# Two layers of cross attention and expert mixtures on one core: routing products in another PSUM bank and place, gathers behind clearing, expert weights split earlier

## The chip, the cores and the metric

The kernel runs on one core of a Trainium2 chip. The metric is the device time of one execution in microseconds. The engines of the core work side by side and wait for each other by semaphores: TensorE (PE in the rows, its weight loads are PEld), VectorE (DVE), ScalarE (ACT), GpSimd (POOL), and SyncE (SP), which only issues transfers.

## The reference

16 batches of 512 tokens with 256 channels go through two layers. Each layer adds a cross attention over 64 context rows and then a mixture of eight experts:

```
x = x + L0_xattn(layernorm(x), ctx, ctx)             # 16 heads of 16
x = x + L0_ffn(layernorm(x))     # router: top 1024 tokens per expert, silu(x Wu) Wd, scatter-add
x = x + L1_xattn(layernorm(x), ctx, ctx, masks)      # the same with two masks
x = x + L1_ffn(layernorm(x))     # every token through all 8 experts, silu(gate) * up, weighted sum
```

In the first mixture a softmax over eight router logits gives each token a gate per expert; each expert takes the 1024 tokens that want it most, so 8 experts times two halves of 512 tokens make 16 groups. Experts of a pair share the up projection (256 to 682), each has its own down projection (682 to 256).

## The kernel before, in words

Nearly every product runs in float32 as three passes: each operand is split into a rounded high part (ACT or DVE) and the remainder (DVE), and PE adds high×high, high×low and low×high (`three_passes`, L143 to L145). There is no scheduler. Each engine has its own program, written out by hand, and the order in that program is the order of execution; `wait_ge(sem, n)` stops everything behind it on that engine.

**Attention** (function `attention`, run once per layer, here 0 and 1). It is pipelined over batches. In the body of batch b, PE does the scores of b (`scores`, L570 to L589, two halves c), the transposes of the input of b+1 (`turn_input`, L530), the output projection of b-1 (`outputs`, L619), the queries of b+1, then four tiles t of weighted values (`weighted_values`, L604) with the maxima products of b+1 between them (`maxima`, L559), the transposes of the new normalised rows of b-1 (`turn_new`, L676), the router logits of b-1 (`route`, L638, eight products), the transposes of the attention result of b (`turn_attention`, L616), and the transposes of the maxima of b+1 (`turn_maxima`, L566). DVE divides each weighted-value tile by its sum (`normalise`, L856 and L858, which signals `av_taken`), reduces the maxima (`maxima`, L844, `s_taken`), copies the turned maxima out (`maxima_copy`, L849, `max_ready`), copies the router logits (`router_copy`, L863, `lg_out`) and takes the remainder of the attention result (`attention_lo`, L868, `a_lo`). ACT takes the exponentials (L736) and high parts (L724 input, L762 attention result). `scores` of the next batch waits for `max_ready`; `turn_attention` waits for the last `av_taken`; `turn_maxima` waits for the last `s_taken`. PSUM has eight banks: weighted values alternate between 6 and 7, outputs use 6 for tiles 0 and 1 and 7 for tiles 2 and 3, the router logits use 6.

**First mixture** (`expert_choice_mixture`). The loop `iterations` runs over q = 0 to 3, one up projection and two experts each; the first three passes share one loop body and the last is written apart. Each q has four groups j of 512 tokens. PE does up(j) (36 products of 512 columns in six chunks f) and, behind it, down(j-1) (72 products of 256 columns); inside up(j), ahead of chunk 2, it turns the rows of group j+1 (`turn`, L1370). POOL gathers the rows by indirect DMA (`gather`, L1316 index copy, L1323) and adds the results back (`add`, L1337), all from one in-order queue. ACT does `hidden`: a Silu per chunk (L1436) and the high parts (L1442 to L1445). DVE takes the remainders (L1493 to L1499), the input's high and low parts (`rows_lo`, L1468 to L1472) after the first remainder of the group before, and the scaled outputs (L1506). There is one raw buffer for a down matrix (`wd`) and two slots for its split form; SP loads the next matrix once `wd_ready` says that DVE has finished the last split (L1296). ACT makes the high part (`down_weights`, L1429), DVE the remainder (L1483). Slot 0 of the next q is split at the end of a q, slot 1 just behind group 0 of its own q.

## Time and profile before

| | us |
|---|---|
| median of 3 runs | 2418.28 (2417.42 to 2419.39) |
| profiled execution, its own time | 2419.39 |
| its span in the profile | 2417.3 |
| PE busy | 2208.7 (91%) |
| DVE busy | 1457.4 (60%) |
| ACT busy | 862.7 (36%) |
| POOL busy | 367.9 (15%) |

The span runs in stages: attention of layer 0 until about 437 us, expert choice to 553 us, the first mixture to 864 us, attention of layer 1 until 1321 us, and the second mixture to the end. Matmuls are pipelined, so a busy PE is not PE at its peak; the starts of the weight loads (PEld) show best when PE goes on to the next piece of work. A bracket at the end of a row tells how long the engine stood idle before it and what released it.

### The profile page before, as it was taken

What the parts mean: (1) busy time and instruction counts of PE and PEld (TensorE: products, weight loads), DVE (VectorE), ACT (ScalarE), POOL (GpSimd) and SP (SyncE); (2) the same over time, 40 slices, a digit from 0 to 9 for tenths busy, and PEclk for the clock granted to TensorE, in tenths of its full rate; (3) what the DMA queues carried; (4) which work ended last, traced back from release to release, by engine and by line L of the source; (5) the groups of instructions that cost most, each with busy time, mean ns of one, the idle gap of its engine ahead of it and who ended that gap; (6) DMA issues with size and microseconds to landing.
All of it is one profiled execution on the core that took longest, in us unless ns stands there. A gap on an engine that the chain in (4) does not pass through costs nothing. (4 is left out here: it accounts for less than half of the span.)

```text
span 2417.3 us, 40461 instructions
## 1 busy us (share of the span) xinstructions
PE 2208.7 (91%) x15335; PEld 1919.7 (79%) x15335; DVE 1457.4 (60%) x3137; ACT 862.7 (36%) x1210; POOL 367.9 (15%) x352
## 2 busy tenths in 40 slices
PE   7999999546999949999996899999999999999998
PEld 4888888325889837788875788888888888888887
DVE  6787876685544447777774774455445554554454
ACT  2455554124544414454442522222222222222222
POOL 3111110105666421111110400000000000000000
PEclk9999999768999969999998999999999999999999
DMA  2121211204444321111112300000000000000000
GB/s 75 53 69 61 78 61 45 65 0 120 100 82 81 44 50 45 61 62 63 57 53 70 114 27 27 27 27 27 1 26 27 27 27 27 27 27 27 27 10 9
DMA packets 110137, 115.05 MB, mean 48 GB/s; under 512 B 16080, under 2 KB 98768, under 8 KB 110032
## 3 DMA queue, kind: packets, MB, share of 16 engines
q1 hardware_dynamic: 97744, 96.49, 12.6%
q0 software_dynamic: 12288, 17.05, 4.2%
q8 instruction: 80, 1.31, 0.2%
q14 instruction: 25, 0.20, 0.0%
HBM read 62.92 MB, written 50.59 MB: 47 GB/s over the span
## 5 line engine op out<-in xcount | busy, mean ns | idle before, releaser
L1882 DVE TENSOR_TENSOR zmix_hid<-zmix_act_gate,psum 128x1024 f32<-128x1024 f32 x128 | 156.4, 1222 | 372.2 <-issue 346.7
L143 PE MATMUL psum<-zmix_wd_hi,zmix_hid_hi 128*128 128x256 f32 x1024 | 289.5, 283 | 2.3 <-DVE zmix_acc L1873 2.3
L145 PE MATMUL psum<-zmix_wd_hi,zmix_hid_lo 128*128 128x256 f32 x1024 | 289.8, 283 | 0.0
L144 PE MATMUL psum<-zmix_wd_lo,zmix_hid_hi 128*128 128x256 f32 x1024 | 289.7, 283 | 0.0
L1833 ACT ACTIVATE zmix_hid_hi<-zmix_hid 128x1024 fp32r<-128x1024 f32 x128 | 135.5, 1058 | 393.3 <-PE psum L145 285.5
L1825 ACT ACTIVATE zmix_act_gate<-psum 128x1024 f32<-128x1024 f32 x128 | 131.6, 1028 | 379.1 <-PE psum L145 379.1
L604 PE MATMUL psum<-att_v_cur,att_probs 128*128 128x96 f32 x2048 | 250.0, 277 | 3.1 <-ACT att_probs L736 3.1
L604 PEld LDWEIGHTS psum<-att_v_cur,att_probs 128*128 128x128 f32 x2048 | 239.1, 192 | 12.0 <-ACT att_probs L736 4.0
L1887 DVE TENSOR_TENSOR zmix_hid_lo<-zmix_hid,zmix_hid_hi 128x1024 fp32r<-128x1024 f32 x128 | 157.8, 1233 | 135.2 <-ACT zmix_hid_hi L1833 134.2
L1873 DVE SCALAR_TENSOR_TENSOR zmix_acc<-psum,zmix_weight,zmix_acc 128x256 f32<-128x256 f32 x512 | 211.7, 476 | 1.6 <-PE psum L145 1.6
L143 PE MATMUL psum<-zmix_xT_hi,zmix_wg_hi 128*128 128x512 f32 x512 | 201.9, 394 | 10.9 <-DVE zmix_xT_lo L1862 10.9
L143 PE MATMUL psum<-zmix_xT_hi,zmix_wu_hi 128*128 128x512 f32 x512 | 200.3, 391 | 4.9 <-DVE zmix_hid L1882 4.7
L143 PEld LDWEIGHTS psum<-zmix_wd_hi,zmix_hid_hi 128*128 128x128 f32 x1024 | 196.0, 191 | 8.7 <-issue 2.0
L144 PE MATMUL psum<-zmix_xT_lo,zmix_wg_hi 128*128 128x512 f32 x512 | 201.6, 394 | 0.0
L145 PE MATMUL psum<-zmix_xT_hi,zmix_wg_lo 128*128 128x512 f32 x512 | 199.9, 390 | 0.0
L144 PEld LDWEIGHTS psum<-zmix_wd_lo,zmix_hid_hi 128*128 128x128 f32 x1024 | 196.0, 191 | 4.8
L144 PE MATMUL psum<-zmix_xT_lo,zmix_wu_hi 128*128 128x512 f32 x512 | 199.8, 390 | 0.0
L145 PE MATMUL psum<-zmix_xT_hi,zmix_wu_lo 128*128 128x512 f32 x512 | 199.7, 390 | 0.0
L145 PEld LDWEIGHTS psum<-zmix_wd_hi,zmix_hid_lo 128*128 128x128 f32 x1024 | 196.0, 191 | 0.0
L736 ACT ACTIVATE att_probs<-psum 128x512 f32<-128x512 f32 x256 | 132.3, 603 | 151.8 <-PE psum L589 79.5
L844 DVE TENSOR_REDUCE att_s_max<-psum 128x8 f32<-128x512 f32 x256 | 163.7, 682 | 30.8 <-PE psum L559 29.5
L143 PEld LDWEIGHTS psum<-zmix_xT_hi,zmix_wg_hi 128*128 128x128 f32 x512 | 97.2, 190 | 28.0 <-DVE zmix_xT_lo L1862 11.1
(295 smaller groups left out, 4502.2 us busy)
## 6 DMA issues: line engine op xcount, KB each, us to landing
x<-att_x_new SPq DMA_DIRECT2D x32, 512.0 KB, 2.9
att_x_in<-in_x SPq DMA_DIRECT2D x16, 512.0 KB, 3.8
rows<-att_normed_new SPq DMA_DIRECT2D x16, 512.0 KB, 3.0
att_x_in<-x SPq DMA_DIRECT2D x16, 512.0 KB, 3.8
turned<-att_newT SPq DMA_DIRECT2D x16, 512.0 KB, 2.8
zmix_xn<-turned SPq DMA_DIRECT2D x16, 512.0 KB, 4.5
zmix_acc<-x SPq DMA_DIRECT2D x16, 512.0 KB, 4.3
out_x<-zmix_acc SPq DMA_DIRECT2D x16, 512.0 KB, 3.2
```

What stands on the lines that cost most here:

```text
L143: pe.matmul(out, st_hi, mv_hi, start=first, stop=False)
L144: pe.matmul(out, st_hi, mv_lo, start=False, stop=False)
L145: return pe.matmul(out, st_lo, mv_hi, start=False, stop=last)
L604: m = pe.matmul(psum[:, 6 + t % 2, cols], probs[:, j, t * P:(t + 1) * P], v_cur[:, p, cols], start=True, stop=True)
L736: act.activation(probs[:, j, :], psum[:, 2 + j % PAIR_ROWS, :], ACT.Exp, scale=DH ** -0.5).then_inc(exp_done, 1)
L844: dve.tensor_reduce(s_max[:, t, :, 2 * c:2 * c + 2], s, AX.X, ALU.max).then_inc(s_taken, 1)
L1825: act.activation(act_gate[:, :, :], psum[:, 0:2, :], ACT.Silu).then_inc(gate_out, 1)
L1833: act.activation(hid_hi[:, e % 2, :, :], hid[:, :, :], ACT.Copy).then_inc(hi_made, 1)
L1873: dve.scalar_tensor_tensor(acc[:, p, t, :], psum[:, 4 + t // 2, (t % 2) * D:(t % 2 + 1) * D], weight[:, bass.ds(b * TT + t, 1), e], acc[:, ...
L1882: dve.tensor_tensor(hid[:, :, :], act_gate[:, :, :], psum[:, 2:4, :], ALU.mult).then_inc(up_out, 1)
L1887: dve.tensor_tensor(hid_lo[:, e % 2, :, :], hid[:, :, :], hid_hi[:, e % 2, :, :].bitcast(F32), ALU.subtract).then_inc(lo_made, 1)
```

## The change

There are two groups of edits. In attention the eight routing products of b-1 go from bank 6 to bank 7, lose one wait, and stand behind the turned maxima instead of ahead of the turned attention result; the wait for `lg_out` in `outputs` goes from tile 0 to tile 2, and on DVE the logits' copy stands behind `attention_lo`. In the first mixture POOL clears the padding rows ahead of its first gather instead of behind it, PE waits for the clearing at its start, and slot 1 of the down weights is split at the end of the q before (for q = 0 ahead of the loop), so that ACT waits there for the last down product of the q.

```diff
             def outputs(b):
                 pe.wait_ge(a_lo, done(KC, b, KC))
                 for t in range(TT):
-                    if t == 0:
+                    if t == 2:
                         after(pe, lg_out, b)
                     for c in range(KC):
                         rows = slice(t * P, (t + 1) * P)
...
                     if t % 2:
                         m.then_inc(o_made, 1)
 
-            def route(b, p, tiles):
-                if 0 in tiles:
-                    pe.wait_ge(new_out, b + 1)
-                    if there(b + 1):
-                        pe.wait_ge(av_taken, done(TT, b + 1, TT - 1))
-                for t in tiles:
+            def route(b, p):
+                pe.wait_ge(new_out, b + 1)
+                for t in range(TT):
                     for c in range(KC):
-                        m = pe.matmul(psum[:, 6, t * PE_COLS:(t + 1) * PE_COLS], newT[:, p, c, t * P:(t + 1) * P], kv["wr"][:, c, :],
+                        m = pe.matmul(psum[:, 7, t * PE_COLS:(t + 1) * PE_COLS], newT[:, p, c, t * P:(t + 1) * P], kv["wr"][:, c, :],
                                       start=(c == 0), stop=(c == KC - 1))
-                if TT - 1 in tiles:
-                    m.then_inc(lg_made, 1)
+                m.then_inc(lg_made, 1)
 
             def body(b, p, half):
                 nxt = there(b + 1)
...
                         turn_new(b - 1, 1 - p)
                     if nxt and t % 2 == 0:
                         maxima(b + 1, 1 - p, t // 2)
-                if there(b - 1):
-                    route(b - 1, 1 - p, range(TT))
                 turn_attention(b)
                 if nxt:
                     turn_maxima(b + 1)
+                if there(b - 1):
+                    route(b - 1, 1 - p)
 
             def turn_new(b, p):
                 pe.wait_ge(norm_out, done(TT, b, TT))
...
             def close(n):
                 outputs(n - 1)
                 turn_new(n - 1, 1)
-                route(n - 1, 1, range(TT))
+                route(n - 1, 1)
             def set_up_and_first():
                 pe.wait_ge(setup["ident_made"], 2)
                 setup["turn_context"](pe)
...
 
             def router_copy(b):
                 dve.wait_ge(lg_made, b + 1)
-                dve.tensor_copy(logits_all[:, bass.ds(b * TT, TT), :], psum[:, 6, 0:TT * PE_COLS].rearrange("p (t e) -> p t e", e=PE_COLS)[:, :, 0:8]).then_inc(lg_out, 1)
+                dve.tensor_copy(logits_all[:, bass.ds(b * TT, TT), :], psum[:, 7, 0:TT * PE_COLS].rearrange("p (t e) -> p t e", e=PE_COLS)[:, :, 0:8]).then_inc(lg_out, 1)
 
             def attention_lo(b):
                 for c in range(KC):
...
                         maxima(b + 1, t // 2, [2 * (t % 2), 2 * (t % 2) + 1])
                 if nxt:
                     maxima_copy(b + 1)
+                attention_lo(b)
                 if there(b - 1):
                     router_copy(b - 1)
-                attention_lo(b)
 
             def close(n):
                 layernorms(n, 0, B // 2, lambda: residual(n - 1, 1, B // 2 - 1))
...
                 for h in range(2):
                     add(e + 1, 1, h)
 
-            for h in range(2):
-                gather(0, 0, h)
             for p in range(2):
                 pool.memset(mid_lo[BIAS_ROW:, p, FC - 1, :].bitcast(F32), 0.0).then_inc(cleared, 1)
                 pool.memset(mid_hi[BIAS_ROW:, p, FC - 1, :].bitcast(F32), 0.0).then_inc(cleared, 1)
...
             for p in range(2):
                 pool.memset(mid_hi[BIAS_ROW:BIAS_ROW + 1, p, FC - 1, :].bitcast(F32), 1.0).then_inc(cleared, 1)
             pool.wait_ge(cleared, 6)
+            for h in range(2):
+                gather(0, 0, h)
             iterations(pool, body)
             for s in range(2):
                 pool.wait_ge(added[s], E * 16 * HT)
...
 
             def down(g, j):
                 p, i = j % 2, j // 2
-                if j == 0:
-                    pe.wait_ge(cleared, 6)
                 pe.wait_ge(lo_made, done(PAIRS + 1, g, PAIRS + 1))
                 for t in range(HT):
                     if t % 2 == 0:
...
                         down(g + j - 1, j - 1)
                 down(g + GJ - 1, GJ - 1)
 
+            pe.wait_ge(cleared, 6)
             turn(0, 0, 0)
             iterations(pe, body)
 
...
                 act.wait_ge(wu_ready, q + 1)
                 for j in range(GJ):
                     hidden(q * GJ + j, j % 2, q * EP + j // 2)
-                    if j == 0:
-                        act.wait_ge(down_made[1], q * (EP * HT))
-                        down_weights(q * EP + 1, 1)
                 if not last:
                     up_weights(q + 1)
-                    act.wait_ge(down_made[1], q * (EP * HT) + HT)
-                    down_weights(q * EP + EP, 0)
+                    for i in range(EP):
+
+                        act.wait_ge(down_made[1], q * (EP * HT) + (i + 1) * HT)
+                        down_weights(q * EP + EP + i, i)
 
             up_weights(0)
             down_weights(0, 0)
+            down_weights(1, 1)
             iterations(act, body)
 
         @block.vector
...
                     else:
                         hidden_lo(q * GJ + j, j % 2, q * EP + j // 2,
                                   None if last else lambda: rows_lo(q * GJ + GJ, 0, q * EP + EP, q + 1))
-                    if j == 0:
-                        down_weights(q * EP + 1, 1)
                     if j >= 1:
                         out(j - 1)
                 if not last:
...
                     dve.wait_ge(down_made[1], q * (EP * HT) + HT)
                     down_weights(q * EP + EP, 0)
                 out(GJ - 1)
+                if not last:
+                    down_weights(q * EP + EP + 1, 1)
 
             up_weights(0)
+            down_weights(0, 0)
             rows_lo(0, 0, 0, 0)
-            down_weights(0, 0)
+            down_weights(1, 1)
             iterations(dve, body)
```

On PE, around the end of a batch in attention of layer 0 (`att_wr_sb` are the router's weights, `att_att` the attention result, `att_s_max` the maxima), before:

```order
L604 MATMUL psum<-att_v_cur,att_probs 128x96 x8
L635 REGISTER_ALU
L638 MATMUL psum<-att_wr_sb,att_newT 128x96 x8
L609 REGISTER_ALU
L616 MATMUL psum<-main_ident,att_att 128x128 x8
L564 REGISTER_ALU
L566 MATMUL psum<-main_ident,att_s_max 128x128 x4
L577 MATMUL psum<-att_qT_hi,att_kb_hi 128x512 x4
```

The same place on PE in the changed kernel (its L635 is L638 of before):

```order
L604 MATMUL psum<-att_v_cur,att_probs 128x96 x8
L609 REGISTER_ALU
L616 MATMUL psum<-main_ident,att_att 128x128 x8
L564 REGISTER_ALU
L566 MATMUL psum<-main_ident,att_s_max 128x128 x4
L635 MATMUL psum<-att_wr_sb,att_newT 128x96 x8
L577 MATMUL psum<-att_qT_hi,att_kb_hi 128x512 x4
```

The routing products now stand directly ahead of the next batch's scores (L577) and no longer between the weighted values (L604) and the two sets of transposes.

On POOL, at the start of the first mixture, in the changed kernel (L1312 and L1319 are L1316 and L1323 of before, where both stand ahead of the memsets):

```order
L1347 MEMSET moe_mid_lo 64x512
L1348 MEMSET moe_mid_hi 64x512
L1347 MEMSET moe_mid_lo 64x512
L1348 MEMSET moe_mid_hi 64x512
L1351 MEMSET moe_mid_hi 1x512 x2
L1312 COPY moe_idx_get<-lists_idx 128x8
L1319 DMA moe_rows<-rows,moe_idx_get 128x264 x8
```

All six memsets are now ahead of the first index copy and the first eight gathers.

On ACT, from the end of a q to the first Silu of the last q, in the changed kernel (L1424 is L1429 of before, where only the first of the two splits stands here):

```order
L1419 ACTIVATE moe_wu_hi<-moe_wu 128x1536
L1450 ISA
L1422 ISA
L1424 ACTIVATE moe_wd_hi<-moe_wd 128x768 x2
L1450 REGISTER_ALU
L1422 ISA
L1424 ACTIVATE moe_wd_hi<-moe_wd 128x768 x2
L1280 REGISTER_ALU
L1280 COMPARE_AND_BRANCH
L1431 ACTIVATE moe_mid<-psum,moe_bu 128x512 x2
```

Two splits now stand between the last high part of a q and the first Silu of the next. Inside the loop that first Silu has a table load ahead of it (before and after alike); ahead of the last q there is none.

## Rows read from the trace of the kernel before

**Rows 1.** Busy time by windows: stretch, length, then busy us (count) per engine.

```profile
197.00:220.16 23.16, 21.98 (x209) 19.65 (x208) 18.67 (x55) 12.28 (x23) 3.97 (x5) 1.00 0.22 69
1127.00:1154.00 27.00, 25.50 (x240) 21.40 (x240) 20.63 (x60) 12.81 (x23) 3.94 (x4) 1.00 0.16 58
```

**Rows 2.** Timeline, layer 0: start us, length, engine, line, count, idle before.

```profile
208.61 1.87 PEld L638 LDWEIGHTS psum<-att_wr_sb,att_newT 128*128 128x128 f32 x16
...
209.19 0.42 DVE L858 TENSOR_TENSOR att_att<-psum,att_recip 128x256 f32<-128x256 f32 x1
...
209.53 1.28 DVE L844 TENSOR_REDUCE att_s_max<-psum 128x8 f32<-128x512 f32 x2
...
210.37 0.91 PEld L616 LDWEIGHTS psum<-main_ident,att_att 128*128 128x128 f32 x8
...
211.24 0.47 PEld L566 LDWEIGHTS psum<-main_ident,att_s_max 128*128 128x128 f32 x4
...
212.08 0.69 DVE L849 CAST att_maxT<-psum 128x512 fp32r<-128x512 f32 x1 [1.27 <-PE psum L566]
...
212.82 0.19 PEld L577 LDWEIGHTS psum<-att_qT_hi,att_kb_hi 32*128 32x128 f32 x4 [1.11 <-DVE att_maxT L849]
...
214.04 2.07 ACT L736 ACTIVATE att_probs<-psum 128x512 f32<-128x512 f32 x4 [1.41 <-PE psum L583]
...
217.06 1.22 DVE L829 TENSOR_TENSOR att_nT_lo<-psum,att_nT_hi 128x1024 fp32r<-128x1024 f32 x1 [1.68 <-ACT att_nT_hi L724]
...
229.39 0.53 PEld L559 LDWEIGHTS psum<-att_kb_hi,att_qT_hi 32*128 32x128 f32 x16 [0.35 <-DVE att_s_max L844]
```

**Rows 3.** Timeline, the same place in layer 1.

```profile
1149.77 1.28 DVE L844 TENSOR_REDUCE att_s_max<-psum 128x8 f32<-128x512 f32 x2
...
1153.14 0.22 PEld L577 LDWEIGHTS psum<-att_qT_hi,att_kb_hi 32*128 32x128 f32 x4 [1.18 <-issue]
```

**Rows 4.** Timeline, the last batch of layer 1.

```profile
1296.94 1.87 PEld L638 LDWEIGHTS psum<-att_wr_sb,att_newT 128*128 128x128 f32 x16
...
1297.52 0.42 DVE L858 TENSOR_TENSOR att_att<-psum,att_recip 128x256 f32<-128x256 f32 x1
...
1300.52 1.29 DVE L868 TENSOR_TENSOR att_aT_lo<-psum,att_aT_hi 128x512 fp32r<-128x512 f32 x2 [1.31 <-ACT att_aT_hi L762]
```

**Rows 5.** Timeline, start of the first mixture, POOL and PE.

```profile
553.92 0.19 POOL L1316 COPY moe_idx_get<-lists_idx 128x8 int32<-128x8 int32 x1 [101.83 <-POOLq L984]
...
563.95 1.57 PEld L1370 LDWEIGHTS psum<-main_ident,moe_rows 128*128 128x128 f32 x8 [10.94 <-DMA moe_rows<-rows,moe_idx_get]
...
565.54 0.52 POOL L1353 MEMSET moe_mid_lo<- 64x512 f32 x1
...
568.98 1.19 POOL L1316 COPY moe_idx_get<-lists_idx 128x8 int32 x1 [0.48 <-POOL moe_mid_hi L1357]
```

**Rows 6.** Issues between 630 and 637 us: size, us to landing (issued at 636.2).

```profile
moe_wd<-in_w_down SPq DMA_DIRECT2D x1, 768.0 KB, 6.4
```

**Rows 7.** Timeline, first change of q in the mixture.

```profile
634.56 1.28 ACT L1436 ACT_TABLE_LOAD   x1 [6.45 <-DVE moe_wu_lo L1479]
...
643.25 1.06 ACT L1442 ACTIVATE moe_mid_hi<-moe_mid 128x1024 fp32r<-128x1024 f32 x1
...
646.81 1.23 DVE L1472 TENSOR_TENSOR moe_xT_lo<-psum,moe_xT_hi 128x1024 fp32r<-128x1024 f32 x1
...
648.65 0.41 PE L143 MATMUL psum<-moe_xT_hi,moe_wu_hi 128*128 128x512 f32 x1
...
650.48 0.95 POOL L1323 DMA_INDIRECT moe_rows<-rows,moe_idx_get  x1 [0.30 <-issue]
...
650.63 1.56 ACT L1429 ACTIVATE moe_wd_hi<-moe_wd 128x768 fp32r<-128x768 f32 x2
652.16 1.27 ACT L1436 ACTIVATE moe_mid<-psum,moe_bu 128x512 f32<-128x512 f32 x2
...
653.31 1.10 PE L1370 MATMUL psum<-main_ident,moe_rows 128*128 128x128 f32 x8 [1.72 <-DMA moe_rows<-rows,moe_idx_get]
```

## The prediction, made before the changed kernel was run

> **What bounds the kernel now.** I read the windows of one batch in each attention first, then the timeline around the moved products, then the starts of the first mixture and of its second q. In attention PE is busy for 22.0 of the 23.16 us of a batch in layer 0 and 25.5 of 27 us in layer 1 [rows 1]. So PE sets the pace, and the reader should look for its few holes. The one that comes in every batch is between the turned maxima and the next scores: 1.11 us in layer 0, 1.18 us in layer 1, while DVE copies the maxima out [rows 2, 3]. In layer 0 there is a second chain of the same length: scores release ACT's exponentials (start 214.04), these hold the input's high part, DVE waits 1.68 us for that and then runs almost without a gap until PE waits 0.35 us for its reduced maxima (229.39) [rows 2]. Whatever delays the scores delays both chains. In the mixture PE waits once at the start, 10.94 us for the first gathered rows [rows 5], and in the second q 1.72 us at the turn of group 2, again for gathered rows [rows 7].
>
> **Attention, the routing products behind the turned maxima.** They add and remove nothing on PE: sixteen records, 1.87 us long, of which 0.11 overlaps with what follows, so 1.76 us [rows 2]. What changes is which wait they cover. Before, PE is free at 208.61, routes until 210.37, turns the attention result (0.87) until 211.24, turns the maxima (0.47) until 211.71, waits 1.11 us, and starts the scores at 212.82. In that order the routing covers two results of DVE: the last divided tile, 209.19 + 0.42 = 209.61, and the last reduced maxima, 209.53 + 1.28 = 210.81 [rows 2].
>
> With the change PE stands at 208.61 before the attention result, which is late: a semaphore costs about 0.05 us (the maxima's copy ends at 212.77, the scores start at 212.82), so it waits until 209.66, 1.05 us. It turns until 210.53, waits for the maxima until 210.86 (0.33), and turns them until 211.33. Routing then takes until 213.09, and the scores are behind it. The copy of the maxima starts 0.84 us after their turn began and takes 0.69, ready at 212.39, so it no longer matters. Scores start at 213.09 instead of 212.82, +0.27. In other words, a hole of 1.11 us is filled and holes of 1.38 us are opened. In layer 1 the maxima end at 1149.77 + 1.28 = 1151.05; 0.05 of semaphore, 0.47 and 1.76 give 1153.33 against 1153.14, +0.19 [rows 3]. The mean is 0.23; a semaphore of PE may well cost 0.1 instead of 0.05, and the change from full-height products to scores in quarters has to follow at once now instead of behind a hole. I take 0.3 and bound it by 0.1 and 0.5. It happens for b = 1 to 14 in both layers: 28 × 0.3 = 8.4 us (2.8 to 14).
>
> The last batch has no maxima. There the attention result is divided at 1297.52 + 0.42 = 1297.94, and its turn starts at 1297.99 instead of 1296.94 + 1.76 = 1298.70, 0.71 earlier; the routing ends by 1300.6, before the remainder that the outputs wait for (1301.81 - 0.71 = 1301.1) [rows 4]. Twice 0.7: -1.4 us.
>
> The logits' copy behind `attention_lo` costs nothing: the routing ends at 213.1, about when DVE finishes the remainders, and what follows on DVE has 1.68 us of waiting ahead of the input's low part [rows 2] (if that cover went, 0.2 us a batch). The wait for `lg_out` at tile 2 is met by then, nothing gained either. Attention: +7.0 us.
>
> **Start of the first mixture.** The memsets begin at 565.54 and the next index copy at 568.98, 3.4 us for the piece that now stands ahead of the first gather; about 0.4 of it is the entry to the loop, which stays behind. So the first index copy goes from 553.92 to about 556.9. Everything behind is a chain: four gathers, the landing, PE's turn at 563.95 [rows 5]. Bounds: 1.5, if the transfers land faster once the weights have passed, and 4.5, if the index copy or a gather falls beside a DVE split (the second copy took 1.19 us beside one, the first 0.19 [rows 5]). I take +3.0. DVE's first split now ahead of the input's parts is hidden in this wait, as is slot 1's: ACT would finish it by about 573, before the first up chunk of the later start.
>
> **Changes of q.** Slot 1 of the next q is split on ACT behind slot 0, before that q's first Silu. Its raw matrix is issued at 636.2 and lands at 642.6 [rows 6]; the split takes 1.56, until 644.2. The table load ahead of the first Silu, which ran at 634.56 in idle time, now comes behind it: 1.28, until 645.5. Two Silus and their high part take 1.27 + 1.06, until 647.9, against 643.25 + 1.06 = 644.3 before. The input's low part of the next group follows 3.7 us behind (646.81 + 1.23 = 648.04 against 644.3): 651.6. PE began that up product at 648.65 and so waits 3 us there. It reached the turn of group 2 at 653.31 - 1.72 = 651.6, 2.9 after 648.65; now it gets there at 654.5. The old wait for rows swallows the rest: +1.2 us [rows 7]. POOL, whose last gather of those rows is issued at 650.48 [rows 7], also gets DVE's split beside its index copy and the next down matrix on the transfer engines: 0.3 more. The first two changes have the table load, the third has none, and without its 1.28 PE arrives as the rows do: 0.2 + 0.3. Sum 1.5 + 1.5 + 0.5 = 3.5 us (0 to 9: 0 if all stays within the old wait, 3 each if nothing is swallowed). Taking slot 1's split out of group 0 to 1 frees ACT at 650.63, but PE does not wait there, so nothing comes back.
>
> The Trainium skill, page ScalarE: Activation LUTs, section What ACT_TABLE_LOAD costs, says that a load to another set costs about 1.28 us and a drain of about 1.38 us with it. The trace has the 1.28 and shows no drain; by the page the first two changes of q would each cost 1.38 more, and the sum would be 2.8 higher.
>
> **Sum.** 7.0 + 3.0 + 3.5 = +13.5 us. Against the profiled execution's own 2419.39 this is 2432.9; the median of the runs is 1.1 lower, and I forecast 2431.8.
>
> **Rivals.**
> *The routing fills the hole and the scores come earlier.* If routing took no longer than PE's slack, the scores would start when the maxima are ready, 212.39 instead of 212.82: 28 × -0.43 = -12.0, less 1.4, plus 3.0 and 3.5: -6.9, 2411.4, faster. For it speaks that the hole is there in every batch. Against it speaks its size: from the end of the turned maxima (211.33) to that copy are 1.06 us, and 1.76 us of products have to go in. It decides at a routing of under 1.1 us. 5%.
> *Little of it shows.* Attention at 0.1 a batch (2.8 - 1.4), the start at 1.5, no loss at a change of q: +2.9, 2421.2, within the bound. For it: the terms per batch are differences of numbers ten times larger, and the layer 1 row gave only 0.19. Against: the products stand at both places in full, and the memsets have nothing to hide behind. 9%.
> *POOL sets the change of q.* If the gathers of group 2 are pushed by a DVE split of 1.75 us on top of PE's delay, each change costs about 3: +9 instead of 3.5, 2437.3. For it: the copy that took 1.19 beside a split instead of 0.19 [rows 5]. Against: most gathers beside remainders of DVE keep 0.95 us. 15%. The Trainium skill, page SBUF — State Buffer, section Who interferes with whom, has it that a DVE instruction with two SBUF inputs contends with a GpSimd instruction that reads SBUF; the copy agrees.
> *The loads of the table bring a drain.* As above, 2434.6. 7%.
> The forecast itself: 64%.
>
> **How the numbers follow.** A measurement tells about 0.2% of this kernel, 4.8 us, from no change. Slower by more: the forecast, the third and the fourth rival, 86%; the forecast's lower edge is still above the bound. Within: 9% and a little of the forecast's weight, 10%. Faster: 4 to 5%, 4%. The range leaves out the first rival and the end of the second, and goes up to where the attention term is 0.45 or the changes of q cost 3 each: 2424 to 2441.
>
> **What would show it.** In the profile after, in layer 0: a wait of about 1.05 us ahead of the turned attention result and one of 0.3 ahead of the turned maxima, none ahead of the scores, and a batch of 23.45 us instead of 23.16. In layer 1 27.0 should go up by as much. PE's first turn in the mixture at about 3 us more behind the block's start, and at the changes of q a new wait of some 3 us for the input's low part, with the wait for rows gone or smaller. I am wrong if the scores still wait for the copied maxima (the routing is then shorter than I read), if the period of a batch is unchanged, or if the mixture's end shifts by less than 3 us.

## The result and the profile after

The change makes the kernel slower, as forecast: median 2433.68 us (2430.27 to 2435.78, 4 runs) against 2418.45 us (2417.42 to 2419.39, 4 runs), ratio 1.0061, 95% interval 1.0044 to 1.008. That is 15.2 us more; the forecast was 2431.8 us, 13.5 more. The profiled execution took 2435.47 us, its span is 2433.4.

First part of the page after (before: PE 2208.7, DVE 1457.4, ACT 862.7, POOL 367.9). DVE and ACT have hardly moved. PE is busy 11.2 us longer with the same 15335 products, 6.3 of it in the first mixture (280.52 to 286.77), so the new time is partly waiting and partly products that take longer. POOL is busy 6.5 us longer, 5.3 of it in the first mixture:

```profile
PE 2219.9 (91%) x15335; PEld 1921.7 (79%) x15335; DVE 1457.9 (60%) x3137; ACT 862.1 (35%) x1210; POOL 374.4 (15%) x352
```

I cut both spans at the same instructions. The first mixture goes from SP's first weight load to the first load of attention 1; in attention the period is that of DVE's copy of the turned maxima.

| | before | after |
|---|---|---|
| period of a batch, layer 0 (14 periods) | 23.19 | 23.49 |
| period of a batch, layer 1 (15 periods) | 25.51 | 25.75 |
| first mixture | 310.26 | 322.76 |
| of it, start to the turn of group 4 | 62.39 | 65.25 |
| of it, turn of group 4 to turn of group 8 | 71.17 | 73.37 |
| of it, turn of group 8 to turn of group 12 | 71.15 | 75.37 |
| of it, turn of group 12 to the end | 105.55 | 108.77 |

Stages that the change doesn't touch differ by up to 3.5 us between profiled executions (the first copy of the maxima comes at 72.9 us before and at 69.4 after), so a whole-kernel difference of that size says nothing by itself. Inside the first mixture the rows repeat better: the turn of group 4 comes 62.39, 62.41 and 62.28 us behind the stage's start in the profiles of before, att_only and half_route, and at 65.25, 65.22 and 65.33 in those with the memsets first (the changed kernel, mix_only, gather_only).

**Attention.** Timeline of the changed kernel around the moved products, layer 0 (it answers to [rows 2]; its L616, L566, L577 are those of before, L635 is the routing):

```profile
207.42 0.42 DVE L854 TENSOR_TENSOR att_att<-psum,att_recip 128x256 f32<-128x256 f32 x1
207.76 1.28 DVE L840 TENSOR_REDUCE att_s_max<-psum 128x8 f32<-128x512 f32 x2
207.90 0.86 PEld L616 LDWEIGHTS psum<-main_ident,att_att 128*128 128x128 f32 x8 [0.97 <-DVE att_att L854]
...
209.09 0.42 PEld L566 LDWEIGHTS psum<-main_ident,att_s_max 128*128 128x128 f32 x4 [0.34 <-DVE att_s_max L840]
...
209.48 1.87 PEld L635 LDWEIGHTS psum<-att_wr_sb,att_newT 128*128 128x128 f32 x16
...
209.88 0.69 DVE L845 CAST att_maxT<-psum 128x512 fp32r<-128x512 f32 x1 [0.84 <-PE psum L566]
...
211.44 0.19 PEld L577 LDWEIGHTS psum<-att_qT_hi,att_kb_hi 32*128 32x128 f32 x4
```

The hole ahead of the scores is gone (L577 has no bracket) and two others stand in its place, 0.97 and 0.34 us. From the routing's start to the scores are 1.96 us where the forecast had 1.76: scores in quarters follow the full-height products with 0.2 us between.

**Start of the first mixture.** POOL and PE in the changed kernel (answers to [rows 5]; the memsets were behind the gathers before):

```profile
554.37 0.52 POOL L1347 MEMSET moe_mid_lo<- 64x512 f32 x1 [103.20 <-POOLq L980]
...
557.39 0.19 POOL L1312 COPY moe_idx_get<-lists_idx 128x8 int32<-128x8 int32 x1
558.57 1.18 POOL L1319 DMA_INDIRECT moe_rows<-rows,moe_idx_get  x1 [1.00 <-POOL moe_idx_get L1312]
...
561.32 2.15 POOL L1319 DMA_INDIRECT moe_rows<-rows,moe_idx_get  x1 [0.30 <-issue]
```

PE's first turn starts at 566.59, 11.94 us behind the stage's start; before it was 563.95, 9.76 behind. The last of the four gathers that it needs is issued by 564.71, and the turn follows 1.88 us later; before these were 560.05 and 3.90. So the landing makes up for 2 us, and the gather of 2.15 us instead of 0.95 takes 1.2 of them back.

**A change of q** (the end of one pass of the loop and the start of the next), the second one, in the changed kernel: ACT, DVE and POOL.

```profile
718.40 1.58 ACT L1424 ACTIVATE moe_wd_hi<-moe_wd 128x768 fp32r<-128x768 f32 x2 [13.62 <-DMA moe_wd<-in_w_down]
720.00 1.28 ACT L1431 ACT_TABLE_LOAD   x1
721.29 1.26 ACT L1431 ACTIVATE moe_mid<-psum,moe_bu 128x512 f32<-128x512 f32 x2
```

```profile
720.01 1.76 DVE L1478 TENSOR_TENSOR moe_wd_lo<-moe_wd,moe_wd_hi 128x1536 fp32r<-128x1536 f32 x1 [2.72 <-ACT moe_wd_hi L1424]
...
726.21 1.22 DVE L1467 TENSOR_TENSOR moe_xT_lo<-psum,moe_xT_hi 128x1024 fp32r<-128x1024 f32 x1
```

```profile
718.38 1.55 POOL L1333 DMA_INDIRECT x<-moe_y,moe_idx_add  x1 [0.30 <-issue]
720.23 2.97 POOL L1333 DMA_INDIRECT x<-moe_y,moe_idx_add  x1 [0.30 <-issue]
724.41 1.47 POOL L1319 DMA_INDIRECT moe_rows<-rows,moe_idx_get  x1 [1.00 <-POOL moe_idx_get L1312]
726.18 0.97 POOL L1319 DMA_INDIRECT moe_rows<-rows,moe_idx_get  x1 [0.30 <-issue]
727.46 1.93 POOL L1319 DMA_INDIRECT moe_rows<-rows,moe_idx_get  x1 [0.30 <-issue]
729.69 0.95 POOL L1319 DMA_INDIRECT moe_rows<-rows,moe_idx_get  x1 [0.30 <-issue]
```

And PE's weight loads there, a wait for the input's low part, then one for the gathered rows:

```profile
727.56 0.19 PEld L143 LDWEIGHTS psum<-moe_xT_hi,moe_wu_hi 128*128 128x128 f32 x1 [2.50 <-ACT moe_mid L1431]
...
732.59 0.98 PEld L1366 LDWEIGHTS psum<-main_ident,moe_rows 128*128 128x128 f32 x8 [2.43 <-DMA moe_rows<-rows,moe_idx_get]
```

Two chains are late at once. ACT waits 13.62 us for the landing of slot 1, splits it, loads its table, and only then does the Silus. DVE's remainder of slot 1 runs beside POOL's last add, which takes 2.97 us instead of 1.55, and a gather beside the next remainder of DVE takes 1.93 instead of 0.95. One such slow add stands at each change in the kernel before, too, beside the remainder of the up weights:

```profile
632.62 1.76 DVE L1479 TENSOR_TENSOR moe_wu_lo<-moe_wu,moe_wu_hi 128x1536 fp32r<-128x1536 f32 x1
632.85 2.96 POOL L1337 DMA_INDIRECT x<-moe_y,moe_idx_add  x1 [0.64 <-DVE moe_y L1506]
```

The change adds a second at two of the three changes (2.71 and 2.97 us); at the third the last add begins 0.16 us ahead of the remainder and keeps its 1.56. The waits of the three changes are 2.27 + 0.76, 2.50 + 2.43 and 1.48 + 2.46 us, 11.9 in all; before there was one each, 2.15, 2.17 and 2.20, 6.5 in all. Then comes something that the forecast didn't have. Windows of the changed kernel behind the second wait of this change (columns: length, then busy us of PE, PEld, DVE, ACT, POOL, then PEclk, the granted clock, then DMA share and GB/s):

```profile
731.00:733.00 2.00, 0.41 (x4) 0.41 (x5) 0.51 (x1) 1.37 (x2) 1.70 (x2) 1.00 0.51 129
733.00:734.00 1.00, 1.00 (x8) 1.00 (x7) 0.80 (x2) 0.00 (x0) 0.70 (x2) 0.63 0.35 89
734.00:736.00 2.00, 2.00 (x6) 1.51 (x6) 1.96 (x2) 0.00 (x0) 1.68 (x3) 0.50 0.38 114
736.00:737.00 1.00, 1.00 (x5) 0.79 (x4) 0.49 (x1) 0.43 (x1) 0.09 (x1) 0.67 0.44 114
737.00:739.00 2.00, 2.00 (x10) 1.65 (x9) 0.00 (x0) 1.15 (x3) 1.70 (x2) 1.00 0.22 59
```

The granted clock falls to 0.50, the level of 1.2 GHz, for about 3.4 us. The work lost is the sum of (1 - clock): 0.37 + 1.0 + 0.33 = 1.7 us, an estimate. The rows bear it out: the same products, from the turn of group 2 to the turn of group 3, take 18.73 us here and 17.14 before, 1.6 more.

```profile
751.32 1.03 PEld L1366 LDWEIGHTS psum<-main_ident,moe_rows 128*128 128x128 f32 x8
```

```profile
724.46 0.86 PEld L1370 LDWEIGHTS psum<-main_ident,moe_rows 128*128 128x128 f32 x8 [2.17 <-DMA moe_rows<-rows,moe_idx_get]
...
741.60 1.02 PEld L1370 LDWEIGHTS psum<-main_ident,moe_rows 128*128 128x128 f32 x8
```

(The first row is of the changed kernel, the other two of the one before.) Such a stretch stands at all three changes of q in the changed kernel (from 655, 733 and 808). At the first it comes behind the wait of 2.27 us alone, ahead of the one of 0.76. Before there is none, and the windows at the same place read 1.00:

```profile
722.00:724.00 2.00, 0.73 (x4) 0.26 (x2) 1.82 (x3) 2.00 (x4) 1.70 (x2) 1.00 0.51 135
724.00:726.00 2.00, 1.53 (x11) 1.46 (x12) 1.37 (x2) 1.65 (x3) 1.65 (x2) 1.00 0.24 68
```

### The profile page after: what moved, and what is told of

It reads as the page before. It is cut to its first block and busy times, and to the rows that moved or that the text cites. A ratio compares the mean times of both kernels' runs of the same rounds, so it can differ in the third digit from the quotient of the medians.

```text
span 2433.4 us, 40395 instructions
## 1 busy us (share of the span) xinstructions
PE 2219.9 (91%) x15335; PEld 1921.7 (79%) x15335; DVE 1457.9 (60%) x3137; ACT 862.1 (35%) x1210; POOL 374.4 (15%) x352
## 3 DMA queue, kind: packets, MB, share of 16 engines
q8 instruction: 80, 1.31, 0.2%
## 5 line engine op out<-in xcount | busy, mean ns | idle before, releaser
L604 PE MATMUL psum<-att_v_cur,att_probs 128*128 128x96 f32 x2048 | 252.7, 278 | 4.5 <-ACT att_probs L732 3.1
L604 PEld LDWEIGHTS psum<-att_v_cur,att_probs 128*128 128x128 f32 x2048 | 240.8, 193 | 14.6 <-ACT att_probs L732 4.0
L1333 POOL DMA_INDIRECT x<-moe_y,moe_idx_add x64 | 107.2, 1674 | 89.3 <-DVE moe_y L1501 72.5
```

Of the source, the lines that this page charges most:

```text
L604: m = pe.matmul(psum[:, 6 + t % 2, cols], probs[:, j, t * P:(t + 1) * P], v_cur[:, p, cols], start=True, stop=True)
L1333: pool.indirect_dma_start(x, at, y[:, h, t, :], None, compute_op=ALU.add).then_inc(added[h], 16)
```

## The experiments

All times are medians with the ratio to the kernel before and its interval; the median of before was 2417.2 to 2417.9 us. The last two columns are readings of one profiled execution each.

| | us | ratio | first mixture in the profile | stretches at 0.5 at the changes of q |
|---|---|---|---|---|
| att_only | 2424.39 | 1.0031 (1.002 to 1.0042) | 310.12 | 0 |
| mix_only | 2425.76 | 1.0038 (1.0026 to 1.005) | 319.71 | 2 |
| gather_only | 2419.70 | 1.001 (1.0001 to 1.0019) | 313.48 | 0 |
| split_only | 2424.49 | 1.0033 (1.0021 to 1.0045) | 316.26 | 1 |
| act_early | 2428.26 | 1.0042 (1.0028 to 1.0055) | 322.82 | 2 |
| split_filler | 2424.83 | 1.0036 (1.0022 to 1.005) | 318.13 | 0 |
| split_two_raw | 2432.63 | 1.0059 (1.0046 to 1.0073) | 324.50 | 3 |
| act_early_two_raw | 2422.60 | 1.0016 (1.0007 to 1.0025) | 316.48 | 1 |
| att_last | 2416.13 | 0.9992 (0.9983 to 1.0001) | 311.04 | 0 |
| half_route | 2404.59 | 0.9946 (0.9933 to 0.996) | 310.31 | 0 |
| half_two_raw | 2402.47 | 0.9937 (0.9923 to 0.9951) | 311.89 | 0 |
| half_warm | 2400.72 | 0.9926 (0.9912 to 0.994) | 309.85 | 0 |

**att_only and mix_only: the two halves of the change.** The edit of each is the attention part, or the mixture part, of the change's diff.

> The kernel before with the attention edits of the change alone (route behind the turned maxima, bank 7, router copy behind the remainders); both mixtures as before. Theory (as forecast, and as the trace after shows it): each batch but the last costs 0.3 us more, the last of a layer less, net +5 to +7 us, 2423 to 2425 us. The last batch gains 2.3 us of it by the trace after, because PE no longer idles 2 us before the outputs and its granted clock stays at 1.0 there (before it read 0.5 to 0.6 for 4 us). Rival (route fills the hole ahead of the filled scores): faster, about 2413 us. Rival (the attention edits do nothing, all is in the mixture): 2418 us.

> The kernel before with the mixture edits of the change alone (memsets ahead of the first gathers, slot 1 of the down weights split early); attention as before. Forecast on record: +6.5 us (3.0 start, 3.5 changes of q), 2425 us. The trace after reads +12.5 us for the first mixture, 2431 us, if that stage is as long without the attention edits. Rival: part of the 12.5 us comes from the attention edits through the clock or the state of the queues, then 2425 to 2428 us.

The medians give +6.6 and +8.0 us; their sum, 14.6, is the 15.2 of the whole within the scatter, so no interaction of the halves is seen, within the several us that the two intervals leave. In att_only the periods are 23.48 and 25.77 us and the first mixture is unchanged. mix_only's first mixture is 9.5 us longer than before, not 12.5; a stage's length is a reading of one execution, and mix_only's runs go from 2422.8 to 2431.6 (the profiled one is the fastest of them).

**att_last: the routing behind the attention result in the last batch alone.** Looking at the two traces I had seen that before, in layer 0, the clock reads 0.61 and 0.54 from 418 to 422 us, at the output products behind the last attention, right behind a wait of 2.25 us, and that it stays at 1.00 there in the changed kernel, where that wait is 0.41 us:

```profile
418.38 0.26 PEld L143 LDWEIGHTS psum<-att_wo_hi,att_aT_hi 128*128 128x128 f32 x1 [2.25 <-DVE att_aT_lo L868]
```

The edit (not shown: bank 7 there, and DVE's copy of the logits behind the remainders):

```diff
-                if there(b - 1):
+                if there(b - 1) and nxt:
                     route(b - 1, 1 - p, range(TT))
                 turn_attention(b)
+                if there(b - 1) and not nxt:
+                    route(b - 1, 1 - p, range(TT), 7)
```

> The kernel before, with the route moved behind turn_attention in the last batch of each layer alone (in bank 7 there); all other batches as before. Clock theory: PE idles less than 1 us at a stretch before the outputs of batch 14 and 15, the granted clock stays at 1.0, and each layer ends 2.3 us earlier: -4.6 us, 2413.8 us. Rival without the clock: only the 0.7 us per layer by which turn_attention comes earlier, -1.4 us, 2417 us. Rival: nothing, 2418.3 us.

1.65 us less, with an interval from -4.1 to +0.2: that leaves out the clock theory's -4.6 but can't tell the rival's -1.4 from nothing. The traces can, for layer 0: from the last copy of the maxima to the first issue of expert choice it is 43.53 us here, 44.17 before and 44.28 in mix_only. The fall of the clock did go from 418 us, but one came earlier, behind PE's wait of 2.09 us for the exponentials of the last batch (windows of att_last):

```profile
402.00:404.00 2.00, 0.99 (x6) 0.99 (x7) 1.60 (x11) 1.45 (x3) 0.00 (x0) 0.84 0.75 251
404.00:406.00 2.00, 2.00 (x11) 2.00 (x11) 1.30 (x9) 0.39 (x1) 0.00 (x0) 0.50 0.04 8
```

mix_only, whose attention is that of before, has it at 402 to 406 too and none at 418, behind the same wait of 2.24 us. So that fall moves between executions, and the last batch's own gain is near the 0.7 us a layer that the forecast gave it.

**half_route: the routing in two pieces.** With a hole on either side of the transposes, half of the products fits each. The edit stands on top of att_last, and DVE's copy of the logits goes behind the remainders in every batch:

```diff
                 if there(b - 1) and nxt:
-                    route(b - 1, 1 - p, range(TT))
+                    route(b - 1, 1 - p, range(2))
                 turn_attention(b)
...
                 if nxt:
                     turn_maxima(b + 1)
+                if there(b - 1) and nxt:
+                    route(b - 1, 1 - p, range(2, TT))
```

> As att_last, and in every other batch the route is cut in two: tiles 0 and 1 (0.88 us of PE) stay ahead of turn_attention, tiles 2 and 3 go behind turn_maxima into the hole of 1.1 us ahead of the filled scores; bank 6 for both, the router copy behind attention_lo. Theory (both holes are filled, turned maxima start about 0.5 us earlier because they are then bound by DVE's s_taken): 28 x 0.4 to 0.5 = 11 to 14 us less, with the last batches 2402 to 2405 us. Rival (the period of a batch is set by DVE's and ACT's chain and not by the place of the route): the same as att_last, 2414 us. Rival (the cut opens new waits as in the change): slower than before, 2420 us or more.

13.2 us less, with periods of 22.76 and 25.09 us (14 and 15 of them make 12.4 us). The rows of PE in layer 0 show why (L638 is the routing, eight records a half):

```profile
206.36 0.97 PEld L638 LDWEIGHTS psum<-att_wr_sb,att_newT 128*128 128x128 f32 x8
207.41 0.86 PEld L616 LDWEIGHTS psum<-main_ident,att_att 128*128 128x128 f32 x8
208.61 0.42 PEld L566 LDWEIGHTS psum<-main_ident,att_s_max 128*128 128x128 f32 x4 [0.34 <-DVE att_s_max L848]
209.00 0.97 PEld L638 LDWEIGHTS psum<-att_wr_sb,att_newT 128*128 128x128 f32 x8
210.14 0.19 PEld L577 LDWEIGHTS psum<-att_qT_hi,att_kb_hi 32*128 32x128 f32 x4 [0.17 <-DVE att_maxT L853]
```

PE waits 0.51 us here where it waited 1.11 before and 1.31 after the change. The scores start when the copied maxima are there, and these now depend on DVE's reductions, no longer on PE.

**gather_only and split_only: the halves of the mixture part.**

> The kernel before with the six memsets of POOL ahead of the first gathers (and PE's wait for them ahead of its first turn) alone; slot 1 and attention as before. Forecast term: +3.0 us (1.5 to 4.5) at the start of the first mixture, 2421 us, and nothing at the changes of q. The trace after reads the first turn of PE 2.2 us later behind the start of the stage. Rival (the bulk of the first mixture's +12.5 us comes from here): +8 us or more. Rival (the gathers wait for the raw weights' transfers anyway): 0, 2418 us.

> The kernel before with the early split of slot 1 alone (ScalarE and DVE ahead of the next q's first hidden layer); gathers and attention as before. Forecast term: +3.5 us, three changes of q, 2421 to 2422 us. Theory from the trace after: each of the 3 changes costs 1.5 to 2.2 us of longer PE waits, and 3.5 to 4 us behind them, in those executions in which the wait falls so, the granted clock reads 0.5, 1.7 us more each: first mixture +6 to +10 us, 2424 to 2428 us, with more scatter than before. Rival (POOL's add and gather beside DVE's remainder are the cause, clock beside the point): +9 us without a stretch at clock 0.5.

+1.8 us (interval 0.2 to 4.6) and +6.6 (5.1 to 10.9): the gathers' 3.0 is inside its interval, and in the profile the turn of group 4 comes 2.9 us later; the split costs nearly twice its forecast. Part of that is not at the changes of q: at the start ACT waits 6.77 us for slot 1, PE 1.01 us for ACT, and group 4 is turned 1.3 us later than before. split_only's trace has a wait of 2.79 us at the first change and no stretch at 0.5, waits of 0.43 and 2.94 us at the second with such a stretch behind them (1.7 us of lost work), and 0.99 and 2.80 us at the third without one.

**act_early: ScalarE's copies early, DVE's remainder of slot 1 at its old place.** The edit against split_only (DVE's order ahead of the loop is that of before, too):

```diff
-                if not last:
-                    down_weights(q * EP + EP + 1, 1)
...
+                    if j == 0:
+                        down_weights(q * EP + 1, 1)
```

> As split_only, but DVE's part of slot 1 (the remainder, 1.76 us) stays at its old place behind the first hidden layer of the next q; ScalarE's copies alone are early. If DVE's remainder beside POOL's adds and gathers makes the rows and xT_lo late: most of split_only's cost goes, +1 to +2 us, 2419 to 2420 us, and PE waits no longer than before for xT_lo. If ScalarE is what costs (it waits for the landing of slot 1 and reloads its table ahead of the first Silu): nearly all of split_only's cost stays, 2423 us or more.

+10.3 us, so DVE's remainder alone is not what costs in split_only; of the adds there, only the last one of the third change is slowed by it. In act_early the last five adds at the second change take 1.55 us each, and PE waits all the same:

```profile
730.27 0.19 PEld L143 LDWEIGHTS psum<-moe_xT_hi,moe_wu_hi 128*128 128x128 f32 x1 [2.94 <-ACT moe_mid L1436]
```

It is even slower than split_only, partly because at the very start, too, ACT waits 10.64 us for slot 1 (the raw buffer is released later) and PE 2.20 and 1.35 us with it, with a third stretch at 0.5 behind that; group 4 is turned 4.7 us later than before. The rest is at the changes of q, where the profile has one stretch more than split_only's and a wait for rows of 4.30 us at the third. The profiled execution was the slowest of five.

**split_filler: PE kept busy in its waits.**

```diff
+                if fill:
+                    pe.wait_ge(silu_made, g * FC - 1)
+                    filler(2, fill)
                 pe.wait_ge(xT_ready, g + 1)
```

`filler` is a number of transposes of the identity into a bank that is overwritten next; eight stand here for j = 1 and eight ahead of the wait for rows of j = 2.

> As split_only, with 8 transposes of the identity that nothing reads ahead of PE's wait for xT of group j = 1 and 8 ahead of its wait for the rows of group j = 2, in each q. Where PE would wait they cost nothing, in the first q, without such waits, 2 x 1.7 us. Clock theory: no stretch at clock 0.5 in the changes of q, 1.7 us less at each where split_only has one, so split_only +3.4 - (2 or 3) x 1.7, about the same as split_only or 2 us less, and in the trace the second and third change 1.7 us shorter each. Rival (the drop has nothing to do with PE's waits): drops as in split_only, and the whole 3 to 10 us slower than it.

The time is split_only's, +0.3 us. In the trace no stretch at 0.5 is left at any change of q; at the second:

```profile
722.00:724.00 2.00, 0.90 (x9) 0.86 (x9) 1.97 (x3) 1.97 (x4) 1.39 (x3) 1.00 0.81 281
724.00:726.00 2.00, 2.00 (x11) 1.66 (x10) 2.00 (x3) 0.80 (x2) 1.70 (x2) 1.00 0.46 125
726.00:728.00 2.00, 2.00 (x16) 1.79 (x15) 0.33 (x1) 1.46 (x3) 1.50 (x2) 1.00 0.29 82
```

The mixture is 1.9 us longer than in split_only. The expected sum, +3.4 for the fillers in the first q and -1.7 for the one stretch that split_only's profile has, gives nearly that, but by luck: up to the turn of group 4 the fillers cost 0.8 us, because split_only waits there too, and behind it 1.1, although the stretch is gone. That the stretches are gone fits a clock that follows PE's waits; as split_only's own profile has only one, this pair alone doesn't prove it, and half_warm below is the cleaner test. As a cure it doesn't pay.

**split_two_raw: a raw buffer for each slot.** It takes the landing out of ScalarE's way:

```diff
-        wu, wd = sc.sb("wu", [P, KC, FP]), sc.sb("wd", [P, FC, D])
+        wu, wd = sc.sb("wu", [P, KC, FP]), sc.sb("wd", [P, EP, FC, D])
...
-                after(sp, wd_ready, e)
+                after(sp, wd_ready, e - 1)
```

> As split_only, with a raw buffer of its own for each slot of the down weights, so that SyncE issues the load of slot 1 long before the change of q. Theory now (ScalarE's wait for the landing of slot 1, ahead of its table load and first Silus, is what costs): the wait of 13.4 to 14.5 us of ScalarE for that DMA goes; what is left ahead of the first Silu is 3.1 us of copies and the 1.28 us table load behind PE's last down product, against 4 tiles of the next group (5.5 us), so PE's wait for xT_lo of group 1 falls from 2.8 us to 1 us or less and no stretch at clock 0.5 stands there: first mixture 310 to 312 us, the kernel 2418 to 2420 us. Rival (ScalarE's extra 3.1 us of copies ahead of the Silus alone is the cost, landing or not): PE still waits 2 us or more, 2423 to 2425 us.

Both expectations fell: +15.4 us. The first half of the theory held, PE's wait for the low part goes to 0.51 us. But now PE waits for the rows, 3.88, 3.86 and 4.82 us, with a stretch at 0.5 behind it at all three changes:

```profile
653.27 0.19 PEld L143 LDWEIGHTS psum<-moe_xT_hi,moe_wu_hi 128*128 128x128 f32 x1 [0.51 <-ACT moe_mid L1439]
...
659.74 1.57 PEld L1373 LDWEIGHTS psum<-main_ident,moe_rows 128*128 128x128 f32 x8 [3.88 <-DMA moe_rows<-rows,moe_idx_get]
```

```profile
646.10 2.82 POOL L1340 DMA_INDIRECT x<-moe_y,moe_idx_add  x1 [0.30 <-issue]
```

Against split_only's profile the mixture is 8.2 us longer. The rows give three parts: PE's waits at the changes of q are 13.6 us instead of 10.0; there are two stretches at 0.5 more, 3.2 us; and group 4 is turned 1.2 us later. The waits grow because DVE's remainder of slot 1, no longer held up by the landing, now runs beside an add at every change (2.82, 2.84 and 2.81 us) and not at one of three.

**act_early_two_raw: the same with DVE's remainder back at its old place**, the DVE edit of act_early on split_two_raw.

> As split_two_raw, with DVE's remainder of slot 1 back at its old place (the DVE side of act_early, the raw buffers of split_two_raw). POOL theory: in split_two_raw PE's new wait of 3.9 us at the turn of group j = 2 is for rows that POOL gathers late, because POOL's seventh add is issued beside DVE's early remainder (2.82 instead of 1.56 us) and the gathers behind it are slowed too; without that remainder the wait is 2 to 2.5 us, as the 2.15 us of before, with no stretch at clock 0.5 behind it, and the kernel falls from 2432.6 to 2418 to 2421 us. Rival (what makes the rows late is the place of the raw loads or ScalarE's early copies, not DVE): the wait stays above 3 us and the kernel above 2428 us.

10 us less than split_two_raw, and POOL's last adds are back to 1.56 us (the one slow add of before stays). The wait for rows is 2.68 us at the first change and 2.60 at the second, a little above the forecast of the theory, one stretch at 0.5 is left, and the kernel ends 1.6 us above the range that I gave; the direction is settled. With the landing gone and the remainder at its old place the kernel is still 4.8 us slower than before (interval 1.7 to 6.0). The profile has 3.6 us from the turn of group 4 on, 1.6 in the stretch at 0.5 and 2 in longer waits, and 2.6 ahead of that turn, of which some 1.4 are the second buffer's (below):

```profile
654.58 0.85 PEld L1373 LDWEIGHTS psum<-main_ident,moe_rows 128*128 128x128 f32 x8 [2.68 <-DMA moe_rows<-rows,moe_idx_get]
```

The four kernels make a square, each with the early high part of slot 1 (time over before, from the table):

| | one raw buffer | two raw buffers |
|---|---|---|
| DVE's remainder early | +6.6 (split_only) | +15.4 (split_two_raw) |
| DVE's remainder at its old place | +10.3 (act_early) | +4.8 (act_early_two_raw) |

Neither step has a price of its own. Moving the remainder back does not help with one buffer (the intervals of split_only and act_early overlap, so it is not shown to harm either) and is worth 10.6 us with two; the second buffer costs 8.8 us with the remainder early and is worth 5.5 with it back.

**half_two_raw and half_warm.** half_two_raw is half_route with the two raw buffers; half_warm is half_two_raw plus this:

```diff
+            warm(7, 20)
             turn(0, 0, 0)
+            warm(7, 6)
```

where `warm` is the filler above.

> half_route with the two raw buffers of split_two_raw, slot 1 split at its old place. The landing of slot 1 is not waited for there, so the second buffer alone should be worth 0: 2404 to 2405 us, as half_route. Rival (the earlier loads collide with the gathers' rows at the start or at the changes of q): +1 to +3 us. It is the control for split_two_raw, since it shows what the second buffer is worth without the early split.

> half_two_raw, with 20 transposes of the identity that nothing reads ahead of PE's first turn of the first mixture and 6 behind it, both in time in which PE waits. Before and in every kernel of this study the granted clock there reads 0.5 until 4.5 us of PE's first up product have gone by; if it follows what PE has just done, it reads 1.0 from the first product on and the stage is 2 us shorter: 2400.5 us. Rival (fillers of this kind don't lift the clock, or it is the wait of the first rows and nothing else that counts): 2402.5 us, as half_two_raw; or 1 us more where they run past the landing of the rows.

The second buffer shows no cost in the time: the median is 2.1 us lower than half_route's, with overlapping intervals. In the profiles it has one, the rival's: both raw loads are now under way with the first gathers, and PE's first turn comes 11.03 to 11.14 us behind the stage's start in the four kernels with two buffers, 9.56 to 9.97 in the seven with one buffer and the gathers first. That is some 1.3 us, which the split experiments with two buffers carry too. With the fillers the clock reads 1.00 at the first products (first fence half_two_raw, second half_warm):

```profile
560.00:562.00 2.00, 1.95 (x5) 1.57 (x6) 1.58 (x1) 0.00 (x0) 1.26 (x1) 0.50 0.00 0
562.00:564.00 2.00, 2.00 (x7) 1.57 (x6) 0.00 (x0) 0.69 (x1) 1.12 (x2) 0.53 0.39 86
```

```profile
560.00:562.00 2.00, 1.50 (x7) 1.25 (x8) 2.00 (x2) 0.00 (x0) 1.52 (x2) 1.00 0.04 8
562.00:564.00 2.00, 2.00 (x13) 1.70 (x12) 0.03 (x1) 1.13 (x2) 1.05 (x2) 1.00 0.30 30
```

PE's first turn stands at 11.03 us in both, the second at 20.05 without the fillers and 18.29 with them, so 1.8 of the 2.0 us by which the stage is shorter arise just there, where the clock differs. The median is 1.75 us lower, in line with it, though the two intervals overlap. half_warm, 0.9926 of before, is the fastest kernel of the study.

## Why the prediction was right, step by step

- *The holes of attention.* Right in kind and size: forecast 1.05, 0.33 and no wait ahead of the scores, read 0.97, 0.34 and none. Forecast 0.3 us a batch; the periods grew by 0.29 in layer 0 (23.45 forecast, 23.49 read) and 0.24 in layer 1. The allowance over the bare difference of 0.23 was due: the scores follow the routing after 1.96 us, not 1.76.
- *The period of layer 1.* The forecast's 27.0 us is not a batch: the window of [rows 1] is longer than one. The period is 25.51 us; the sum doesn't use it.
- *The last batch.* -1.4 us forecast, -1.65 measured with att_last (interval from -4.1 to +0.2, so not told from nothing by the time); layer 0's rows have 0.6 to 0.75 of it.
- *Attention as a whole.* +7.0 forecast, +6.6 measured.
- *Start of the first mixture.* +3.0 forecast, +1.8 measured (interval 0.2 to 4.6, which holds the forecast). In the profile it is 2.2 at PE's first turn and 2.9 at the turn of group 4. The memsets take the 3 us (554.37 to 557.39), but from the index copy to PE's first turn are then 9.2 us (557.39 to 566.59) instead of 10.0 [rows 5]: the landing is faster, as the lower bound has it, and a gather slower, as the upper bound has it.
- *Changes of q.* The step that was mis-sized: +3.5 forecast, +6.6 measured with split_only (interval 5.1 to 10.9), and 9.6 in the profile of the changed kernel from the turn of group 4 on. ScalarE's chain came as worked out: slot 1 landed at 644.8 (forecast 642.6, on a turn that itself was 3.3 us later), and PE waited 2.27, 2.50 and, without the table load, 1.48 us where I had 3 and 1.7. What failed is "the old wait for rows swallows the rest". It took only part of it at the first change (0.76 left) and nothing at the other two (2.43 and 2.46 against 2.17 and 2.20 before), because POOL is later by about as much as PE. I had put DVE's work beside POOL at 0.3 us; the last add is 1.2 and 1.4 us longer at two changes, and the four gathers of group 2 take 5.3 us in all instead of 3.9 at the first. The other part was not in the sum at all, the stretches at 0.5 of the clock, 1.6 us each by the rows. The two parts close the account: 5.4 us of waits and 4.8 of clock make 10.2 against 9.6 read.
- *The third rival, POOL sets the change of q*, had the right mechanism for part of this. split_two_raw and act_early_two_raw differ in the place of DVE's part alone: 3.88 and 2.68 us of waiting at the first change, 10 us in the time. act_early shows that it is not the whole cause.
- *The fourth rival, a drain with the table load.* Not seen: the load runs from 720.00 to 721.28 and the Silu starts at 721.29. The Trainium skill, page ScalarE: Activation LUTs, section What ACT_TABLE_LOAD costs, gives a drain of about 1.38 us with it; here, behind copies that ACT itself had just finished, the trace has none.
- *The first rival*, routing that fills the hole and brings the scores forward, failed for this change. The gain that it saw is there with half of the routing in each hole, 13.2 us with the last batch.
- *The upper edge of the range*, 2441, takes both an attention term of 0.45 a batch and 3 us at each change of q, not one of them, as the text has it.

The two errors of the sum were of opposite sign in part (-1.2 at the start, +3.1 at the changes of q, -0.4 in attention), so that 13.5 stands against 15.2. That the total came out closer than its largest miss is luck; a good total does not prove its terms.

Open: why one wait is followed by the lower clock and a like one is not. In split_only waits of 2.79 and 2.80 us had none behind them and one of 2.94 had, in act_early_two_raw 2.68 had and 2.60 had none, in the changed kernel 2.27 had, and in the last batch of attention 2.09 had in att_last and 2.24 had none in mix_only.

## What to carry to other kernels

Where one piece of work covers a wait, look on both sides of its new place: moving it whole trades one hole for others, and half in each may fill both. Two chains that are late at the same point hide each other, and removing one (split_two_raw) can show the other in full or move it beside something worse; that says nothing against the diagnosis, so take both away together. Price a longer wait of PE not only by its length but by the products behind it, which may run at half clock, and look at several executions: a fall of the clock moves from place to place between them.

## What the runs showed of the hardware that I had not expected

- The granted clock fell to 0.50 for 3 to 4 us behind waits of 2.09 to 4.82 us in an otherwise busy PE, at a cost of 1.6 us each (18.73 us instead of 17.14 for the same products); other waits of 2.07 to 2.80 us had no fall behind them, the single ones of 2.15 to 2.20 us at the changes of q of the kernel before among them. With transposes of no use in the waits no fall was left (split_filler), and ahead of a stage they brought the clock up before its first products (half_warm, 1.8 us).
- POOL's issue of an indirect DMA took 2.97 us beside a subtraction of DVE with both inputs in SBUF, 1.55 alone, and a gather 1.93 instead of 0.95. What is added is a little less than what was left of the subtraction when POOL began: 1.42 of 1.54 us, 1.15 of 1.28 (the add of 2.71 us at the first change) and 0.98 of 1.11 (the gather). The Trainium skill, page SBUF — State Buffer, section Who interferes with whom, has it that such an instruction of DVE contends with GpSimd's reads, and infers that descriptor generation is spared; the traces here agree with the first (an index copy took 1.19 instead of 0.19 us [rows 5]) and speak against the inference. split_only has one add that began 0.04 us ahead of DVE's subtraction (643.01 against 643.05) and kept its 1.56 us, which fits the page's sentence that the order of issue decides who blocks.
